# Attention layers: where the two x tiles are transposed in a slot

## The reference

```
q, k, v = heads(x @ Wq + bq), heads(x @ Wk + bk), heads(x @ Wv + bv)
probs   = softmax(q @ k.T / sqrt(64) + where(adj, 0, -9e15))
ctx     = merge_heads(probs @ v)
x       = layernorm(x + ctx @ Wf + bf)
```

## Time and profile before

| | |
|---|---|
| median of 3 runs | 3063.09 us |
| profiled execution | 3062.43 us |
| its span, first to last instruction | 3060.6 us |
| TensorE busy | 2962.0 us (97%) |
| weight loads | 2625.7 us (86%) |
| VectorE busy | 2554.9 us (83%) |
| ScalarE busy | 2410.0 us (79%) |
| POOL busy | 1255.3 us (41%) |
| mean granted TensorE clock | 0.993 |

### The profile page before, as it was taken

One profiled execution on the slowest core, in us unless ns is written; L12 is line 12 of the kernel. 1 busy time (PEld: TensorE's weight loads), 2 busy tenths in 40 slices (PEclk: granted clock), 3 DMA queues, 4 the chain that ended last, 5 costly groups with the idle time before them and its releaser, 6 DMA issues. The chain is left out here.

```text
span 3060.6 us, 72407 instructions
## 1 busy us (share of the span) xinstructions
PE 2962.0 (97%) x22432; PEld 2625.7 (86%) x22432; DVE 2554.9 (83%) x8621; ACT 2410.0 (79%) x6924; POOL 1255.3 (41%) x1239
## 2 busy tenths in 40 slices
PE   7999999999959999999999999999999999999997
PEld 6888888888748999989899898999989899998986
DVE  5888888888848888888888888888888888888887
ACT  6999999999947777777777777777777777777775
POOL 2666666666632333232233433323232332323223
PEclk9999999999979999999999999999999999999999
DMA  2111110111022222222233222222222222222221
GB/s 80 35 35 35 35 35 30 34 35 35 25 87 68 79 73 74 75 75 78 69 100 84 72 78 75 75 72 79 71 75 78 70 80 73 73 76 75 77 70 54
DMA packets 153211, 198.83 MB, mean 65 GB/s; under 512 B 48896, under 2 KB 115456, under 8 KB 152320
## 3 DMA queue, kind: packets, MB, share of 16 engines
q1 hardware_dynamic: 152832, 194.20, 23.1%
HBM read 68.31 MB, written 50.33 MB: 39 GB/s over the span
## 5 line engine op out<-in xcount | busy, mean ns | idle before, releaser
L967 POOL TENSOR_TENSOR a_residual<-a_x,a_br 128x384 f32<-128x384 f32 x192 | 191.1, 1018 | 1395.5 <-DVE a_mix L1157 1380.0
L1038 ACT ACTIVATE a_probs<-a_logits,a_nmax 128x256 f32<-128x256 f32 x1152 | 572.9, 503 | 5.9 <-DVE a_nmax L1129 3.6
L89 PE MATMUL a_pj<-a_xt_hi,a_w_lo 128*128 128x256 f32 x1728 | 500.5, 290 | 7.0 <-DVE a_xt_lo L1110 6.2
L91 PE MATMUL a_pj<-a_xt_hi,a_w_hi 128*128 128x256 f32 x1728 | 485.5, 281 | 0.0
L90 PE MATMUL a_pj<-a_xt_lo,a_w_hi 128*128 128x256 f32 x1728 | 485.3, 281 | 0.0
L1129 DVE CUSTOM_DVE_ANT_0 a_logits<-a_s,a_mask 128x256 f32<-128x256 f32 x1152 | 432.8, 420 | 5.9
L349 ACT ACTIVATE g_exps<-g_v,g_nmax 128x256 f32<-128x256 f32 x768 | 386.0, 519 | 3.2
L1150 DVE TENSOR_SCALAR a_probs<-a_probs,a_recs 128x256 f32<-128x256 f32 x1152 | 356.8, 352 | 20.4
L1023 ACT ACTIVATE a_split<-a_pj,a_bc 128x256 fp32r<-128x256 f32 x576 | 239.7, 467 | 166.3 <-PE a_pj L91 166.3
L1031 ACT ACTIVATE a_stack<-a_split 64x512 fp32r<-64x512 f32 x576 | 360.7, 626 | 3.4
L89 PEld LDWEIGHTS a_pj<-a_xt_hi,a_w_lo 128*128 128x128 f32 x1728 | 325.7, 188 | 8.9 <-issue 6.8
(11 more groups left out here) (119 smaller groups left out, 8101.3 us busy)
## 6 DMA issues: line engine op xcount, KB each, us to landing
a_stack<-a_split SPq DMA_DIRECT2D x576, 128.0 KB, 2.3
a_x<-y SPq DMA_DIRECT2D x96, 384.0 KB, 3.1
y<-a_out SPq DMA_DIRECT2D x96, 384.0 KB, 2.7
g_x<-x SPq DMA_DIRECT2D x32, 384.0 KB, 3.1
y<-g_out SPq DMA_DIRECT2D x32, 384.0 KB, 2.5
w_stage<-att_w SPq DMA_DIRECT2D x3, 2304.0 KB, 11.5
a_adj<-adj SPq DMA_DIRECT2D x96, 64.0 KB, 3.1
g_adj<-adj SPq DMA_DIRECT2D x32, 64.0 KB, 3.0
```

The lines of the kernel that those rows point to most:

```text
L89: pe.matmul(out, a[1], b[0], start=first, stop=False)
L91: return pe.matmul(out, a[0], b[0], start=False, stop=last)
L1038: last = act.activation(probs[:, (HEADS * u + h) % 4, t, :], logits[:, h % 2, t, :], ACT.Exp, scale=-1.0, bias=nmax[:, u, h, t:t + 1], acc ...
```

## The change

In TensorE's slot, the contexts of the previous sample's pair 0 move behind both transposes of x, and so stand right in front of the contexts of pair 1. In ScalarE's slot, `high_ct(prev, 0)` moves behind `high_xt` 0 and 1 accordingly. VectorE's, POOL's and SP's lists stay as they are.

```diff
@@ ScalarE's slot
                 if cur:
                     own_rows(*cur, 1)
-                if prev:
-                    high_ct(*prev, 0, prev_layer)
                 if nxt:
                     high_xt(*nxt, 0)
                     high_xt(*nxt, 1)
+                if prev:
+                    high_ct(*prev, 0, prev_layer)
                 if cur:
                     own_rows(*cur, 2)
@@ TensorE's slot
                 _, nxt_layer, prev_layer = layers
-                if prev:
-                    pair_of_contexts(*prev, 0)
                 if nxt:
                     transpose_x(*nxt, 0, opening)
                     transpose_x(*nxt, 1, opening)
                 if prev:
+                    pair_of_contexts(*prev, 0)
                     pair_of_contexts(*prev, 1)
                     pair_of_transposes(*prev, 2)
```

## The result

The changed kernel takes 3096.74 us (median of 4 runs, 3096.24 to 3099.11) against 3063.1 us: 1.0109 times as long, 95% interval 1.0092 to 1.0127. The forecast was 3094, slower. The order of work did what the diff says; the time went to one new wait.

The account below looks back on a forecast made before the run. The prediction took TensorE's order in the attention layers as the bound. The uncovered wait, partly repaid by the seams, gave +0.33 us in 94 slots, 31 us on 3063.09: 3094 us, range 3084 to 3112.

Parts of the forecast that it names:

- What bounds the kernel: In the attention layers TensorE is busy 2093.66 of 2094.00 us, so the order on TensorE is the time.
- The seams: TensorE's switches between kinds of matmul: contiguous contexts would, without a wait, save 0.31 us per slot, 29 us over 94.
- The uncovered wait: x tile 1 waits for VectorE's add_back 1, no longer covered by contexts: +0.33 us per slot net, ends 0.31 and 0.57.
- The idle gap: New idle time on TensorE in front of x tile 1: about 0.45 us, 0.61 in starts.
- ScalarE's cushion: ScalarE's idle time ahead of high_qk(0), 1.34 us before the change, would still be about 1.2 us.
- The count: The change reorders 94 slots; 94 by 0.33 us is 31 us.
- A: Rival: tile 1's wait is hidden and the seams' gain remains, 3034 us, faster; chance 0.05.
- B: Rival: gain and loss balance within 0.2% of 3063, by a smaller gap or later idle time taking up the delay; chance 0.04.
- C: Rival: restart also stalls the contexts, or ScalarE's cushion is used up; 0.6 per slot or more, 3119 and above; chance 0.09.
- D: Rival: TensorE's clock falls; one in twenty of 94 slots at 1.2 GHz would add 105 us, 3200; chance 0.02.
- the prediction's last sum: Chances left outside the forecast's range: 0.09 below it (A and B), 0.10 above it (C and D).

Follow-up runs that it names:

- ScalarE's part alone: Only ScalarE's list changed against the kernel before, TensorE's left as it was; 3066.61 us, ratio 1.0004.
- the other bank: Changed kernel, but x tile 1 goes into the odd bank of the probabilities' transposes and VectorE makes xt_lo ahead of the statistics; 3036.46 us, ratio 0.991.
- the extra copy: One more VectorE copy of 384 PSUM columns ahead of add_back 1: added to the changed kernel 3142.88 us, to the kernel before 3066.61 us.

## Why the prediction was right

- **What bounds the kernel.** TensorE's order in the attention layers. Right: every run's time follows its period, and ScalarE's part alone changed nothing.
- **The seams.** Forecast 0.31 us a slot, had there been no wait; the other bank shows 0.29 (periods 22.37 and 22.08). Right, and a run showed it rather than a sum.
- **The uncovered wait.** Forecast: tile 1 starts 0.08 after add_back's end, contexts 0.45 later, transposes of the probabilities 1.87 later, +0.33 in all. Measured: 0.05, 0.48, 1.88, +0.34 in that slot and +0.33 as the median of the periods. The small errors cancel: the release was just under the lower end that I had given (0.06), and the restart a little dearer, since tile 1's first two transposes stand 0.16 apart. That spacing is no mark of a wait: behind contexts the kernel before has it too, between 1505.65 and 1505.81.
- **One row read wrong.** I put the start of tile 1 in the kernel before at 1505.92. The row at 1506.14 shows the fifth and sixth transposes, so tile 1 begins with the fourth, one spacing ahead of it:
```profile
1506.03 0.49 PE L1232 MATMUL a_pj<-a_ident,a_x 128*128 128x128 f32 x3
```
Its first transpose has 0.63 us of cover and not 0.52. The forecast did not suffer, since no term of the sum uses it. The expectation for the extra copy in the kernel before did use 0.52, and came out by luck: the weight load, which carries the wait, starts at 1505.92.
- **The idle gap.** 0.45 forecast, 0.42 measured; in starts 0.61 forecast, 0.58 measured. The price follows the starts: the run with another bank puts the whole wait at 0.63 us a slot (3.44 less 2.81), of which the seams pay back 0.29.
- **ScalarE's cushion.** Forecast 1.2 us left ahead of high_qk, measured 1.24. But one thing I did not see: xt_lo starts ahead of where I had it (1518.05, against 1518.24 by my sum), since it follows the statistics directly. In the kernel before, xt_hi of tile 0 came later, behind high_ct, and held xt_lo back by 0.11 after them. It is without effect, for make_qk waits in neither kernel.
- **The count.** 94 slots by 0.33 gave 31; the 92 that I measured between fixed points gave 30.8. The medians differ by 33.6, and I can't say how much of the last 2 to 3 us is the graph stage's own variation.
- **The rivals.** A would have needed the wait to be hidden; it was not, though its number (3034) is what the other bank reached (3036.46). B is out: nothing later in the slot took up the delay. C: neither part came true. The contexts follow tile 1 0.48 after its start, and the cushion held. With ScalarE's old order another path did cost 0.50: xt_hi, and so xt_lo, late for make_qk. C did not name it. D: with an idle gap of 0.42 us in each of 90 slots the granted clock was 1.00, in the extra copy's kernel with 0.88 as well. The Trainium skill (TensorE: Matmul & The Clock Gate, "A second HAM failure mode: psum-queue depth-cycling") tells of another kernel whose micro-idles between matmul groups made the clock swing. That did not show here; the measurement decides. The chances of C and D add up to 0.11, where the prediction's last sum has 0.10.

## What to carry to other kernels

When TensorE is never idle, work that seems to stand in the wrong place may be cover: before moving it, look up when the next instruction's buffer comes free, and on which engine's end that depends. A reorder that saves seams and opens a wait should be split in two by the question whether the buffer can be another one; here that turned +1.1% into -0.9%. And the reader behind a moved producer needs its cover too: put too late, x cost more than put too early.

## What I had not expected of the hardware

A switch between kinds of matmul has a price that depends on the pair. I read it off starts, from the last matmul of the old kind to the second of the new one, beyond the normal spacings (0.17 and 0.12 for products of 384 and 256 columns, 0.11 for transposes, 0.22 for a pair of contexts):

| from, to | beyond the normal spacing, us |
|---|---|
| product, transposes | 0 |
| transposes, product | 0 |
| product, contexts | 0.09 + 0.05 |
| transposes, contexts | 0.09 + 0.05 |
| contexts, transposes | 0.10 + 0.05 |
| contexts, product | 0.10 + 0.10 |

The first term is at the switch itself, the second in the first spacing of the new kind. Contexts behind contexts, and transposes behind transposes, pay nothing. The table adds up to the runs: the change takes away one switch from a product into contexts and one from contexts into transposes, 0.14 + 0.15 = 0.29, which is what the other bank gained.

The release of TensorE by VectorE took 0.05 to 0.06 us in all 93 slots of each of the three runs in which tile 1 waited, where the weight load itself carries the wait. For make_qk, behind a separate wait, it took 0.14 (both contexts ahead of both tiles).
